# Layout and order: four heads' lines of Q and K put side by side in DRAM, an order of work planned with the queue of transfers, and experts' weights asked for later

## What is computed

```python
h = _layernorm(x, axis=-1) * (1 + ca) + sa
x = x + ga * _L0_attn_ref(h, ...)       # 16 heads of 8 features, softmax over 512 keys
h = _layernorm(x, axis=-1) * (1 + cb) + sb
x = x + gb * _L0_ffn_ref(h, ...)        # 8 experts (128-352-128), the best 2 of each row, and a shared one
...
x = x + ga * _L1_attn_ref(h, ...)       # the same heads through a latent of 32, causal
x = x + gb * _L1_ffn_ref(h, ...)        # 8 experts (128-128-128), squared relu, the best 2 of each row
```

## Time and profile before

| | |
|---|---|
| median of 3 runs | 1233.9 us (1233.62 to 1234.98) |
| the profiled execution: time, span | 1241.14 us, 1239.2 us |
| mean granted TensorE clock | 0.928 |
| busy share of PE, DVE, ACT, POOL | 86%, 71%, 60%, 33% |
| mean busy share of the 16 DMA engines, bytes moved | 48.4%, 169.21 MB |
| packets under 2 KB | 103,600 of 133,230 |

### The profile page before, as it was taken

How to read it: one execution, slowest core, us unless ns; L and a number is a source line. 1 busy time by engine, 2 the same in 40 slices (tenths; PEclk the granted TensorE clock), 3 DMA queues, 4 the chain that set the end, 5 groups by cost and what they waited for, 6 DMA issues and landing times.

```text
span 1239.2 us, 22795 instructions
## 1 busy us (share of the span) xinstructions
PE 1067.6 (86%) x8372; PEld 548.8 (44%) x8372; DVE 885.3 (71%) x1809; ACT 743.7 (60%) x1235; POOL 409.2 (33%) x462
## 2 busy tenths in 40 slices
PE   4588988779897888998987998979999798999986
PEld 2121222125454444454454664555666344544454
DVE  5998889868786766877566785658665776777354
ACT  3067868467564655666654654545756575777844
POOL 2000303170214334313344234342115652433352
PEclk9578999879899998999998999979999898999988
DMA  4715262837457448447457485484752715241110
GB/s 121 159 31 138 82 153 72 235 102 179 160 180 193 149 125 212 146 156 211 149 168 179 144 238 166 142 214 157 179 163 69 166 55 114 92 97 48 61 37 17
DMA packets 133230, 169.21 MB, mean 137 GB/s; under 512 B 19248, under 2 KB 103600, under 8 KB 133120
## 3 DMA queue, kind: packets, MB, share of 16 engines
q1 hardware_dynamic: 127808, 156.49, 45.4%
q0 software_dynamic: 4736, 10.49, 3.0%
q10 hardware_dynamic: 576, 0.79, 0.2%
HBM read 109.07 MB, written 58.62 MB: 135 GB/s over the span
## 4 chain that ended last, share of the span: by engine, by line
PE 35%; DMA 21%; DVE 16%; issue 13%; ACT 7%; POOL 6%; SPq 2%; POOLq 0%; DVEq 0%; ACTq 0%
PE ps L687 8%; DMA d_h<-hx,pos 7%; DVE nm L862 7%; DMA gr<-d_y,pos 6%; PE ps L748 4%; PE ps L670 4%; PE ps L649 4%; PE ps L771 3%; ACT ES L1210 3%; PE ps L756 3%; DMA d_u<-US 2%; PE ps L764 2%; ACT xn L1142 2%; POOL gr L1392 1%; DMA DR<-d_r 1%
## 5 line engine op out<-in xcount | busy, mean ns | idle before, releaser
L862 DVE TENSOR_REDUCE nm<-ps 128x2 f32<-128x1024 f32 (+3 forms) x512 | 507.7, 1016 | 97.0 <-PE ps L655 54.3
L1210 ACT ACTIVATE ES<-ps 128x1024 f32<-128x1024 f32 (+3 forms) x512 | 431.4, 863 | 197.0 <-PE ps L670 98.4
L687 PE MATMUL ps<-ES,VS 128*9 128x512 f32 (+3 forms) x2048 | 235.0, 539 | 9.8 <-DVE nmp L873 9.1
L649 PE MATMUL ps<-KS,QS 48*128 48x512 bf16 (+3 forms) x1024 | 186.9, 368 | 53.6 <-DVE nm L862 31.8
L670 PE MATMUL ps<-QS,KS 51*128 51x512 bf16 (+3 forms) x1024 | 181.8, 358 | 43.9 <-DVE nm L862 29.7
L748 PE MATMUL ps<-hsT,wst 128*128 128x128 f32 x1104 | 159.1, 291 | 2.6 <-DVE hdx L1046 2.1
L748 PEld LDWEIGHTS ps<-hsT,wst 128*128 128x128 f32 x1104 | 140.5, 200 | 30.3 <-issue 25.4
L670 PEld LDWEIGHTS ps<-QS,KS 51*128 51x128 bf16 x1024 | 49.6, 95 | 206.0 <-issue 81.0
L649 PEld LDWEIGHTS ps<-KS,QS 48*128 48x128 bf16 x1024 | 50.6, 96 | 183.0 <-DVE nm L862 64.8
L1412 POOL TENSOR_TENSOR ya<-ya,yS 128x512 f32<-128x512 f32 x49 | 62.6, 1277 | 155.6 <-DVE yS L1106 155.4
L1392 POOL DMA_INDIRECT gr<-d_y,pos x64 | 66.5, 1038 | 111.1 <-issue 56.2
(11 more groups left out here) (187 smaller groups left out, 1397.2 us busy)
## 6 DMA issues: line engine op xcount, KB each, us to landing
wst<-we SPq DMA_DIRECT2D x92, 576.0 KB
d_u<-US SPq DMA_DIRECT2D x64, 256.0 KB
KS<-d_k SPq DMA_DIRECT2D x64, 192.0 KB
QS<-d_q SPq DMA_DIRECT2D x64, 192.0 KB
d_q<-sp SPq DMA_DIRECT2D x16, 384.0 KB
d_k<-sp SPq DMA_DIRECT2D x16, 384.0 KB
hs<-d_h SPq DMA_DIRECT2D x20, 256.0 KB, 4.7
d_y<-ys SPq DMA_DIRECT2D x20, 256.0 KB
```

What stands on the lines that cost most here:

```text
L649: mm = eng.matmul(psum[:, bank[u][a], 0:n], QS[m][r:r + KA, pr, 128 * t:128 * t + 128], KS[m][r:r + KA, pr, 0:n], start=True, stop=i < NB)
L687: mm = eng.matmul(psum[32 * a:32 * a + 9, b, q0:S], VS[i % 3][:, j, 4 * g + a, :], ES[(2 * (NT * (NG * i + g) + j) + a // 2) % NES][:, a % ...
L862: eng.tensor_reduce(nm[f][:, :].rearrange("p (a c) -> p a c", a=2)[:, :, 4 * pr + t], ps2("score", i, f, pr, t)[:, :, 0:n], AX.X, ALU.max, ...
L1210: eng.activation(ES[(2 * n + pp) % NES][:, :, 0:S - q0], ps2("bscore", i, f, g, j, pp)[:, :, 0:S - q0], ACT.Exp, scale=SC1 if i >= NB else ...
```

## The change

It has three parts.

1. **Layout.** `d_q` and `d_k` change from [partition, place, token] to [place, partition, token], and the weights' columns are put in another order (`pairs`), so that partitions run by feature, then by parity of the head, then by head pair. Four heads of one stack load are then neighbours in DRAM, and each of 48 partitions is filled by one line of 4 KB where there were four of 1 KB. The stores write the same 1 KB lines to other addresses. Bytes and partitions are those of before.
2. **The plan follows the queue of transfers.** `settle` keeps `moved`, the time at which all transfers issued so far are through, by a table of costs `MOVES`, and adds 1.3 times the backlog to the lag of each further transfer. Tables and `SPREAD` get other values. All of this changes only the order of the lists.
3. **Weights.** `x_w` has an urgency of `u - 0.15`, where it was `u - 0.3`.

```diff
-SHIFT = {"t": -0.16, ..., "pv": 0.16, "f": 0.56, ..., "max": -0.56, ..., "g": -0.57, ...}
+SHIFT = {"t": -0.12, ..., "pv": 0.11, "f": 0.37, ..., "max": -0.38, ..., "g": -0.96, ...}
...
+    MOVES = {"stack": 2.7, "p_store": 3.4, "u_st": 0.8, "u_ld": 1.0, "t_ld": 0.8, "t_gt": 0.8, "x_ld": 1.06, "x_st": 1.06,
+             "x_w": 2.0, "c_h": 3.2, "ld": 1.0, "r_sc": 0.27, "g_ga": 0.27, "d_out": 1.0}
...
-        held, mode = {}, None
+        held, mode, moved = {}, None, 0.0
...
             free[e] = end
+            if k[0] in self.MOVES:
+                begin = end if e == "POOL" else t + 0.3
+                if k[0] != "d_out":
+                    lag += PIPE * max(0.0, moved - begin)
+                moved = max(moved, begin) + self.MOVES[k[0]]
...
+PIPE = 1.3
+WEARLY = 0.15
 SLACK, SWITCH = 0.05, 0.1
 
-SPREAD = 2.4, 2.3
+SPREAD = 2.6, 1.8
...
-                    add("SP", ("x_w", q, j), 0.5, u - 0.3, ...
+                    add("SP", ("x_w", q, j), 0.5, u - WEARLY, ...
...
-        d_q = [dram(f"d_q{i}", [H * DH, 6, S], BF16) for i in range(N)]
-        d_k = [dram(f"d_k{i}", [H * DH, 6, S], BF16) for i in range(N)]
+        d_q = [dram(f"d_q{i}", [6, H * DH, S], BF16) for i in range(N)]
+        d_k = [dram(f"d_k{i}", [6, H * DH, S], BF16) for i in range(N)]
...
-                        eng.dma_start(bass.AP(tensor=to.tensor, offset=to.offset + r * S, ap=[[6 * S, 128], [step * S, reps], [1, S]]),
+                        eng.dma_start(bass.AP(tensor=to.tensor, offset=to.offset + r * 128 * S, ap=[[S, 128], [step * 128 * S, reps], [1, S]]),
...
-                            eng.dma_start(to[m][64 * a:64 * a + KA, :, :], bass.AP(
-                                tensor=of.tensor, offset=of.offset + (8 * a + 4 * f) * KA * S,
-                                ap=[[S, KA], [KA * S, 4], [1, S]])).then_inc(slot(*u), 16)
+                            eng.dma_start(to[m][64 * a:64 * a + KA, :, :].rearrange("k h t -> k (h t)"), bass.AP(
+                                tensor=of.tensor, offset=of.offset + (8 * a + 4 * f) * S,
+                                ap=[[H * S, KA], [1, 4 * S]])).then_inc(slot(*u), 16)
...
-    pairs = _np.arange(128).reshape(8, 2, 8).transpose(1, 0, 2).reshape(128)
+    pairs = _np.arange(128).reshape(8, 2, 8).transpose(2, 1, 0).reshape(128)
```

More of the change, by code:

```diff
@@ L55, in wait_ge @@
             self.seen[sem.name] = value
-SHIFT = {"t": -0.16, "s": 1.02, "p": -0.35, "stack": -0.35, "pv": 0.16, "f": 0.56, "d": 1.41, "x": 1.14, "max": -0.56, "r": 0.28, "rr": 0.28, "u": -0.15, "g": -0.57, "bscore": -0.08, "expo": -0.08}
-LATE = {"d": -0.05, "f": -0.22, "score": 0.1, "rowmax": 0.1, "t": 0.43, "max": 0.24, "g": 0.09, "u": 0.82, "s": -0.1}
-LAST = {"max": -0.08, "r": -0.06, "rr": -0.06, "pv": 0.15, "x": 0.14, "p": 0.05, "stack": 0.05, "d": 0.53, "s": -0.54, "t": -0.05, "u": -0.07}
+SHIFT = {"t": -0.12, "s": 1.02, "p": -0.35, "stack": -0.35, "pv": 0.11, "f": 0.37, "d": 1.41, "x": 1.14, "max": -0.38, "r": 0.26, "rr": 0.26, "u": -0.15, "g": -0.96, "bscore": -0.08, "expo": -0.08}
+LATE = {"d": -0.05, "f": -0.22, "score": 0.12, "rowmax": 0.12, "t": 0.43, "max": 0.24, "g": 0.05, "u": 0.82, "s": -0.66}
+LAST = {"max": -0.05, "r": -0.08, "rr": -0.08, "pv": 0.15, "u": 1.18, "d": 0.19, "score": -0.02, "rowmax": -0.02, "g": -0.13}
 class Plan:
+    MOVES = {"stack": 2.7, "p_store": 3.4, "u_st": 0.8, "u_ld": 1.0, "t_ld": 0.8, "t_gt": 0.8, "x_ld": 1.06, "x_st": 1.06,
+             "x_w": 2.0, "c_h": 3.2, "ld": 1.0, "r_sc": 0.27, "g_ga": 0.27, "d_out": 1.0}
     LAG = {"PE": 0.48, "DVE": 0.31, "ACT": 0.33, "POOL": 0.25, "SP": 1.8}
@@ L353, in plan @@
                     n = NMT * q + j - NST
-                    add("SP", ("x_w", q, j), 0.5, u - 0.3, [("x_reg", q, h), ("x_dn", n // NMT, n % NMT)], lag=3.6)
+                    add("SP", ("x_w", q, j), 0.5, u - WEARLY, [("x_reg", q, h), ("x_dn", n // NMT, n % NMT)], lag=3.6)
                     beside = i + SPREAD[0] + SPREAD[1] * j / NMT
```

## The result

The changed kernel took **1192.3 us**, the median of 4 runs (1188.06 to 1196.3), beside 1234.4 us (1233.62 to 1236.25) of the kernel before: a ratio of 0.966 [0.962, 0.970], faster by 42 us. The forecast was 1218 with a range from 1198 to 1240, so the direction was right, the gain was over twice the 16 us forecast, and the range did not hold it. The profiled execution took 1188.06 us, with a span of 1185.7 us and a mean granted clock of 0.948 (0.928 before).

What follows compares the result with a forecast made beforehand. PE, busy 1067.6 of 1239.2 us, was taken as the bound, leaving 171.6 us idle to win. Terms 0 - 11 - 11 - 6 + 12 = -16 us gave 1225.1 from 1241.1, or 1218 on the median's scale; range 1198 to 1240.

Steps and rivals of the forecast that it cites:

- Packets of 4 KB: Stack loads: fewer, larger packets to the same 48 partitions gain nothing; 0 us, ends -9 and +3.
- the first rival: Stack loads get faster as well, over 280 GB/s, 9 us more gain: 1209 us; chance 0.20.
- ACT's stalls: ACT's waits for `rs` before normalizing batches 5 and 7: new order wins 4 of 9.6 and 7 of 8.3, -11 us.
- Gather combines: DVE's waits for gathers at three PE gaps: later combines win 60% of 18.6 us, -11, ends 0 and -18.6.
- The clock: PE's slow clock behind five gaps: 2 us each, 60% of 10 goes, -6 us, ends 0 and -10.
- What is late next: New DVE waits for transfers elsewhere in the order: six at 2.0 us each, +12 us, ends +4 and +35.
- the five gaps: PE waits between 240 and 661 us of 4.1 and 5.5, 8.3, 6.1, 5.0 and 7.5 us, together 36.5.
- Weights: Experts' weights, 92 transfers asked for 0.15 of a block less early: costed at nothing.
- Start and end: SP's first 40 rows and PE's tail from batch 14 essentially unchanged: 0 us, ends -3 and +3.
- second rival: The order only moves the stalls, 28 us of gain meeting 28 us of new waits: 1234 us; chance 0.18.

Runs made afterwards that it cites:

- e9: Changed kernel with the weights' urgency of the kernel before (`WEARLY = 0.3`, was 0.15): ratio 0.962 to the kernel before.
- e8: Changed kernel with `PIPE = 0.0`, so the plan adds no backlog of transfers; new tables kept: ratio 1.012 to the kernel before.
- e12: Changed kernel with old tables, `SPREAD` and weights' urgency, backlog added only to the lag of scatters and gathers: ratio 0.974 to the kernel before.
- e10: Changed kernel with the old tables, `SPREAD` and weights' urgency, still following the queue: ratio 0.966 to the kernel before.
- e5: Kernel before with only ACT's normalizing of batch 7 moved 3 exponentials later: 1238.2 us against 1240.2, ratio 0.9986.
- e6: Kernel before with 11 of the 32 combines on DVE moved 1 to 5 row maxima later: 1239.6 us, ratio 1.0003.
- e7: Kernel before with both hand moves, ACT's normalizing of batch 7 and DVE's 11 combines, later: 1239.1 us, ratio 0.9986.

## Why the prediction was right or wrong

- **Packets of 4 KB: 0, right.** Layout alone is 0.9975 [0.9948, 1.0002], and the queue's packets are 109,376 as said. The loads ran somewhat faster, 190 GB/s at the very end of the 150 to 190 that I gave, but the first rival, which asked for over 280, fell. A load of 786 KB at 165 GB/s takes 4.8 us, not the 4.6 that I wrote; it changes nothing.
- **ACT's stalls: -11, too small.** Both gaps went in full, 17.9 us (8.3 and 9.6), although ACT still waits 16.3 us for `rs` where I asked for under 15.
- **Gather combines: -11, too small.** All 18.6 us went; the waits for gathers are 24.0 us, under the 30 asked for.
- **The clock: -6, too small.** PE's busy time fell by 13.9 us for the same matmuls, more even than the end of 10 that I gave; between 600 and 700 us the mean clock is 1.00, where it was 0.93, so more than the piece just behind the gap had been slow.
- **What is late next: +12, the step that failed most.** PE's idle time fell by 39.6 us where the five gaps account for 36.5, so on balance nothing came back, and 3.1 us more went. Behind 240 us the profile before has seven other gaps of PE of 2.4 to 3.7 us, together 22.0; the changed kernel has four of 2.6 to 3.6, together 12.6. I had priced six new waits at 2.0 us from the rows of the old order. Counted by row maxima, the changed kernel is 2 us behind at 236 us, 38 ahead at 691 and 53 ahead at 853, and over 40 ahead from there on: some 15 us came between 691 and 853 us, where I had looked for no gain.
- **Weights: 0, right** (e9; PE's L759 waits for no transfer). **Start and end: 0, wrong but within its ends of 3.** PE's first matmul comes 2.5 us later (9.5 for 7.0). It does so in every run whose plan adds the backlog to the plain transfers, and in none of the others (e8, e12, and all with the old plan). I had compared the first rows of SP, and the memsets that moved are DVE's.

Against the terms the measured ones are -36.5 - 3.1 - 13.9 = -53.5 between the spans, and -42 between the medians. My own good ends, -17.9, -18.6, -10 and +4, come to -42.5, which would have given 1191.4; I still drew the range from 1198. The ends have one cause, the time that the plan leaves for landings, as e10 to e12 suggest, and so they tend to fall together. I had treated them as separate risks, and cut each share. That my good ends come within 1 us of the measured time is luck in part, since the +4 among them has the wrong sign and the -10 of the clock is too small.

The experiments also show that the reason was wrong in kind. I took a gap's worth from slack at its own place: so many rowmaxes later, so many us of slack. Moving pieces so at four of the gaps gains 0.1% or nothing in the medians, and under 0.35% by the intervals (e5, e6, e7), and hands the wait on, which was the mechanism of my second rival. The rival did describe a hand-made repair. It did not describe this change, since the plan lays out everything behind a late landing anew, and so leaves the wait less to move to. The right question was not whether the five places have slack now, but whether the model that lays out the order knows the cause of all of them. The rows before said that it did not. They don't say so by the 4.7 us of the earlier trace rows, which are other transfers', but by the earlier trace rows: POOL went on at 241.62 us, 6.2 us after it had issued the scatter it waited for, where the plan had 3.4.

## What to carry to other kernels

Where a planner writes the order, compare its durations and lags with the trace first, and with the late cases rather than the median: one lag that suited the median landing (2.1 us) raised to suit nine in ten (4.7) gained 2.6%, which moving pieces by hand at four gaps didn't. Make sure, too, whose landings a median is: that of a tile can leave out the very transfers that matter. When several stalls have one cause, add their ends together for the range, and ask for each repair whether it is local (its wait will move) or goes through the model (it may all stay gained). An engine's waits that grow, as POOL's did from 116.2 to 146.8 us, say nothing against a change if the engines behind it wait less, as ACT (30.0 to 16.3) and DVE (87.7 to 41.0) did.

## What the runs showed of the hardware

Loads into 48 partitions from 0 or 64 ran at 162 to 174 GB/s, slower than into 32 (214) or 64 (224). Two loads into 96 partitions ran at 247, more than four of 48 that take turns (182); they are also twice as large, so the partitions' share in that isn't separated.

The Trainium skill, page "SBUF — State Buffer", section "Can I just issue two DMAs to hit both halves?", says that two transfers at partitions 0 and 64 gain only 6% over one. By themselves, loads whose halves take turns gained 12% over loads into one half (182 for 162; 7% in the first round, 180 for 168), and 5% over 0, 0, 64, 64. In the kernels the stretch of the first loads gained more than the page's 6%: 170 to 189 GB/s in the kernel before, and 178 and 190 to 217 and 227 in two executions each of the changed one. What I had not expected is that the order of four transfers makes 0.8% of a kernel whose chain names no stack load.
